# Attention and feed-forward layer on one core: half-width score slots, and transposes of the first 12 cells taken two cells at a time

## The reference, cut to what matters

```python
scores = jnp.einsum('bhqd,bhkd->bhqk', q, k) * scale
causal = jnp.tril(jnp.ones((q_len, q_len), bool))
scores = jnp.where(causal[None, None], scores, jnp.asarray(-1000000000.0, dt))
attn = jax.nn.softmax(scores, axis=-1)
out = jnp.einsum('bhqk,bhkd->bhqd', attn, v)
```

## Time and profile before

| what | before |
|---|---|
| median of 3 runs | 2385.06 us (2380.48 to 2385.91) |
| the profiled execution | 2382.02 us |
| its span, first to last instruction | 2380.2 us |
| PE busy | 2369.0 us |
| ACT busy | 1621.9 us |
| DVE busy | 1430.2 us |
| POOL busy | 579.8 us |
| granted TensorE clock, mean | 1.000 |

### The profile page before, as it was taken

The page is one execution under the profiler, slowest core; times in us unless marked ns, Lnnn a source line. Parts: engine busy times, 40 slices in busy tenths (PEclk is TensorE's granted clock), DMA queues, the critical chain, the costliest instruction groups (busy, mean ns, idle before and its releaser), DMA issues.

```text
span 2380.2 us, 41136 instructions
## 1 busy us (share of the span) xinstructions
PE 2369.0 (100%) x12028; PEld 1993.7 (84%) x12028; DVE 1430.2 (60%) x3796; ACT 1621.9 (68%) x3224; POOL 579.8 (24%) x453
## 2 busy tenths in 40 slices
PE   9999999999999999999999999999999999999998
PEld 7888888888888888888888888888888888888887
DVE  5334666666767676766667676766676675242333
ACT  4223878788888888887878888887888885222221
POOL 3002323233332423232323333232323220000000
PEclk9999999999999999999999999999999999999999
DMA  7867444444353444344444445354444345420110
GB/s 272 303 214 290 131 147 138 132 137 149 137 172 106 171 140 146 128 145 139 135 140 141 142 132 164 118 172 123 160 135 145 129 138 194 140 71 36 53 36 18
DMA packets 133271, 340.24 MB, mean 143 GB/s; under 512 B 13344, under 2 KB 30752, under 8 KB 122656
## 3 DMA queue, kind: packets, MB, share of 16 engines
q1 hardware_dynamic: 133216, 339.53, 42.3%
HBM read 232.00 MB, written 111.67 MB: 144 GB/s over the span
## 4 chain that ended last, share of the span: by engine, by line
PE 96%; issue 1%; DVE 1%; ACT 1%; DMA 1%; SPq 0%; POOL 0%; POOLq 0%; DVEq 0%
PE b_ps L267 45%; PE b_sps L267 34%; PE b_tps L1571 10%; PE b_tps L1630 3%; PE b_ps L1630 3%; PE b_tps L267 1%; DMA a_raw<-in_wkrT 0%; PE b_sps L1580 0%; DMA b_kt<-k_d 0%; ACT b_pt L1068 0%; ACT b_sc L1053 0%; ACT b_sc L1047 0%; DVE b_sc L1272 0%; DVE a_xs L1196 0%; POOL a_wkr L930 0%
## 5 line engine op out<-in xcount | busy, mean ns | idle before, releaser
L1290 DVE TENSOR_TENSOR b_pt<-b_tps,b_pt 128x512 fp32r<-128x512 f32 (+3 forms) x768 | 426.7, 556 | 301.5 <-ACT b_pt L1068 297.2
L267 PE MATMUL b_sps<-b_kt,b_qs 128*128 128x512 f32 (+4 forms) x2304 | 497.1, 343 | 0.2 <-DMA b_kt<-k_d 0.2
L1053 ACT ACTIVATE b_sc<-b_sc,b_rinv 128x896 f32<-128x896 f32 (+7 forms) x512 | 396.1, 774 | 105.4 <-DVE b_rinv L1280 98.8
L267 PEld LDWEIGHTS b_sps<-b_kt,b_qs 128*128 128x128 f32 x2304 | 403.2, 188 | 55.6 <-issue 0.9
L1068 ACT ACTIVATE b_pt<-b_tps 128x512 fp32r<-128x512 f32 (+3 forms) x768 | 367.6, 479 | 115.7 <-PE b_tps L1571 113.9
L267 PE MATMUL b_ps<-b_xs,b_wq 128*128 128x512 f32 x1536 | 440.7, 406 | 0.0
L267 PE MATMUL b_ps<-b_pt,b_vt 128*128 128x512 f32 x1584 | 435.9, 402 | 0.3 <-DVE b_ys L1301 0.3
L267 PE MATMUL b_ps<-b_wo,b_ot 128*128 128x512 f32 x1536 | 423.9, 405 | 0.1
L1047 ACT ACTIVATE b_sc<-b_sc,b_nmax 128x896 f32<-128x896 f32 (+7 forms) x512 | 395.4, 772 | 40.1 <-DVE b_nmax L1272 37.0
L1272 DVE CUSTOM_DVE_ANT_0 b_sc<-b_sps,b_mask 128x896 f32<-128x896 f32 (+7 forms) x512 | 386.5, 755 | 16.2 <-PE b_sps L267 16.1
L1571 PE MATMUL b_tps<-b_ident,b_sc 128*128 128x128 f32 x2304 | 374.3, 272 | 1.4 <-DVE b_pt L1290 1.3
(11 more groups left out here) (142 smaller groups left out, 2274.5 us busy)
## 6 DMA issues: line engine op xcount, KB each, us to landing
b_xs<-xs_d SPq DMA_DIRECT2D x32, 2048.0 KB, 9.0
b_ys<-y_d SPq DMA_DIRECT2D x128, 256.0 KB, 2.7
y_d<-b_ys SPq DMA_DIRECT2D x128, 256.0 KB, 3.0
k_d<-a_ks SPq DMA_DIRECT2D x32, 512.0 KB, 3.9
v_d<-a_vs SPq DMA_DIRECT2D x32, 512.0 KB, 3.0
b_kt<-k_d SPq DMA_DIRECT2D x64, 256.0 KB, 4.3
b_vt<-v_d SPq DMA_DIRECT2D x16, 1024.0 KB, 4.8
b_wraw<-in_wqT SPq DMA_DIRECT2D x64, 256.0 KB, 2.8
```

Of the source, the lines that this page charges most:

```text
L267: ins = nc.tensor.matmul(out, *every[n], start=(n == 0), stop=(n == len(every) - 1))
L1053: nc.scalar.activation(sc[:, slot, 0:w], sc[:, slot, 0:w], ACT.Copy, scale=rinv[:, slot:slot + 1])\
L1290: nc.vector.tensor_tensor(pt[:, u, LO, 0:nj, h * P:(h + 1) * P], tps[n % 2][:, 0:nj], pt[:, u, HI, 0:nj, h * P:(h + 1) * P], ALU.subtract) ...
```

## The change

Two things are changed. Cells 0 to 15 get half a slot (512 columns) of `sc` each, so eight of them fit where four did, and DVE waits for the transposes of cell c - 8 in place of c - 4. And the transposes of cells 0 to 11 are made in steps 4, 6, 8, 10, 12 and 14, those of cells c - 1 and c one behind the other, where each had a step of its own (3 to 14). In steps 3, 5, 7, 9, 11 and 13 PE makes scores and fill alone. ACT and DVE take both pieces in the step of the pair, as their jobs 0 and 1. The diff, cut:

```diff
+PAIRED = 12
+
+
+def transposed_in(step):
+
+    if LAG <= step < PAIRED + LAG:
+        return [(step - LAG - 1, 0), (step - LAG, 0)] if (step - LAG) % 2 else []
+    c = step - LAG
+    return [(c, n) for n in range(len(pieces(c % CELLS)))]
...
+PAIR_ORDER = ("scores", 0, 1, "fill")
...
+        def sc_at(c):
+
+            return sc[:, c % S_RING, 512 * (c // GQ % 2):][:, 0:512] if c < 16 else sc[:, c % S_RING]
+
+        def sc_before(c):
+
+            return c - 2 * S_RING if S_RING <= c < 16 else c - S_RING
...
-                dve.wait_ge(t_done, PIECES * it + thru(c - S_RING) + TD0)
+                dve.wait_ge(t_done, PIECES * it + thru(sc_before(c)) + TD0)
...
-                        elif cell := cell_at(step - LAG, it, turn):
-                            hi_pt(*cell, job)
+                        elif job < len(ts := transposed_in(step)) and (cell := cell_at(ts[job][0], it, turn)):
+                            hi_pt(*cell, ts[job][1])
...
-                    ts = pieces(cell[1]) if cell else []
-                    shares = cut(parts, SHARES[len(ts)])
-                    for job in (0, 1, "scores") if step == 0 else PE_ORDER[part_of(step)]:
+                    ts = [(cell, pieces(cell[1])[n]) for c, n in transposed_in(step) if (cell := cell_at(c, it, turn))]
+                    paired = LAG <= step < PAIRED + LAG
+                    shares = cut(parts, (1,) if paired else SHARES[len(ts)])
+                    order = PAIR_ORDER if paired else PE_ORDER[part_of(step)]
+                    for job in (0, 1, "scores") if step == 0 else order:
```

More of the change, by code:

```diff
@@ L1045, in exp @@
                 act.wait_ge(sc_done, CELLS * it + c + 1 + SC0)
-                nc.scalar.activation(sc[:, slot, 0:w], sc[:, slot, 0:w], ACT.Exp, bias=nmax[:, slot:slot + 1],
+                nc.scalar.activation(sc_at(c)[:, 0:w], sc_at(c)[:, 0:w], ACT.Exp, bias=nmax[:, slot:slot + 1],
                                      scale=-1.0, accum_out=rsum[:, slot:slot + 1]).then_inc(exp_done, 1)
@@ L1052, in normalise @@
                 act.wait_ge(rinv_done, CELLS * it + c + 1)
-                nc.scalar.activation(sc[:, slot, 0:w], sc[:, slot, 0:w], ACT.Copy, scale=rinv[:, slot:slot + 1])\
+                nc.scalar.activation(sc_at(c)[:, 0:w], sc_at(c)[:, 0:w], ACT.Copy, scale=rinv[:, slot:slot + 1])\
                     .then_inc(norm_done, 1)
@@ L1270, in mask_max @@
                 w = P * (i + 1)
[L1272 removed]
+                nc.vector.tensor_tensor_reduce(out=like_banks(sc_at(c)[:, 0:w], i), in0=both_banks(sps[c % 2], i),
                                                in1=like_banks(mask[:, S - w:S], i),
@@ L1440, in turn_of @@
                                     add_q(it + g, int(kind == "q1"), a)
-                        elif cell := cell_at(step - LAG, it, turn):
-                            lo_pt(*cell, job)
+                        elif job < len(ts := transposed_in(step)) and (cell := cell_at(ts[job][0], it, turn)):
+                            lo_pt(*cell, ts[job][1])
                             if turn in ("first", "loop") and step - 1 == D_SPLIT[0] and job == 0:
@@ L1570, in transposes @@
                 for j in range(nj):
-                    last = nc.tensor.transpose(tps[n % 2][:, j], sc[:, c % S_RING, (j0 + j) * P:(j0 + j + 1) * P],
+                    last = nc.tensor.transpose(tps[n % 2][:, j], sc_at(c)[:, (j0 + j) * P:(j0 + j + 1) * P],
                                                ident[:])
@@ L1746, in turn_of @@
                     parts = plan_of(turn).spread[step]
-                    here, cell = cell_at(step, it, turn), cell_at(step - LAG, it, turn)
+                    here = cell_at(step, it, turn)
                     if step == 0:
@@ L1760, in turn_of @@
                         elif job < len(ts):
-                            transposes(*cell, ts[job])
+                            transposes(*ts[job][0], ts[job][1])
             def a_all_values(t):
```

## The result

| | before | after |
|---|---|---|
| median of 6 runs each, same chip | 2382.99 us | 2393.72 us (2392.35 to 2394.59) |
| ratio after / before | | 1.0043, 95% interval 1.003 to 1.0056 |
| span of the profiled execution | 2380.2 us | 2392.5 us |

What follows compares the result with a forecast made beforehand. PE was taken as the bound, busy 2369.0 of 2380.2 us. Gains of 1.0 + 1.9 and cost 0 gave 2.9 us: 2379.1 us profiled, 2382.2 us as median, range 2375 to 2388.5 us.

Steps and rivals of the forecast that it cites:

- Part 3: Moved work on ACT and DVE: same instruction counts, the shifted copies covered by 0.71 us at cell 13; cost 0.
- rival B: New wait at cell 13: shifted ACT copies delay `normalise` by over 0.66 us; 20.8 us lost, 2403 us; chance 0.04.
- Part 2: Cell 0's late transpose in step 3 goes, 2.3 us, less 0.4 charged at cell 1; gain 1.9 us, 1.5 to 2.3.
- Part 1: On PE, 96 merged pairs save a transpose-fill border of 0.01 us each; gain 1.0 us, between 0 and 1.9.
- Rival A: A transpose border on PE costs the visible 0.09 us, so merging saves that; 10.5 us gained, 2374.6 us; chance 0.07.
- Rival C: Nothing gained: borders cost 0.00 and step 3's wait moves whole to cell 1; 2385 us; chance 0.17.
- Rival D: PE's clock falls in longer transpose runs, matmuls taking twice the time; 42 us lost, 2424 us; chance 0.02.
- The base of the sum: Starting times on the kernel before: 2382.0 us for the profiled execution, 2385.1 us for the median of the runs.
- if the even steps show a late transpose: Sign against the forecast: transposes starting late in the even steps, where the pairs stand, would prove it wrong.
- the cell 13 check: Sign in the profile after: cell 13's transpose must follow its `normalise` by more than 0.05 us.

Runs made afterwards that it cites:

- e10: The change, with ACT taking both copies of a pair ahead of `exp` in steps 3 to 14; 2385.04 us, ratio 1.0012 to the kernel before.
- e12: The change, with DVE taking the low part of a pair's second piece one step later, behind reciprocal and `add_q`; 2385.91 us, ratio 1.0012.
- e4: The change, with half of step 15's fill put ahead of the transposes of cell 12; 2394.19 us, ratio 1.0045.
- e5: Kernel before, fill of steps 20 to 31 in four shares, one put amid the first piece's four transposes; 2383.78 us, ratio 1.0003.
- e6: Kernel before, fill of steps 20 to 31 in the same four shares, the first piece left whole; 2383.50 us, ratio 1.0003.
- e3: The change with only cells 0 to 7 in pairs, the last two pairs left out; 2384.63 us, ratio 1.0010.
- e11: The change, with both copies of a pair ahead of `exp` on ACT and half of step 15's fill ahead of cell 12's transposes; 2381.90 us, ratio 0.9994.
- e8: Kernel before, with the four high copies of the `wo` weights moved from ACT to POOL; 2401.42 us, ratio 1.0078.
- e9: The change, with half of the fill ahead of the transposes in steps 15 to 18 (cells 12 to 15); 2394.33 us, ratio 1.0044.

## Why the prediction was wrong, point by point

**Part 3 failed, and with it the forecast.** It said: "0.71 us of cover, of which 0.49 and 0.05 are used, 0.17 left. Cost 0." Three things were wrong in that step.

- It looked at one reader only, cell 13's `normalise`. The reader of piece 10 itself was left out: cell 12's transposes need DVE's low part of piece n - 2, and that rule stands in the text on the kernel. Before, it had 3.37 us; one step later it had less than nothing. It could have been charged ahead of the run, as is worked out below this list.
- It said of DVE that "the low part of the second piece stands ahead of the next step's row maximum" and stopped there. What stands directly behind it is reciprocal and `add_q`, and ACT waits for `add_q`. The copy that was put behind `exp` holds DVE for 0.52 us, and DVE then holds ACT, which the rows show as 0.28 of idle time. This happens in steps 13 and 15 (in front of 925.72 and, with the same 0.28, of 932.82) and pushes all of ACT back. The hold is longer than the idle time: the copy of the queries starts 0.87 us behind the copy ahead of it (924.85 to 925.72), and 0.48 in e10 (920.67 to 921.15). The 0.39 between them is nearly the whole of the 0.41 us a turn that e10 and e12 both give back.
- It treated the 0.49 of the moved copy as the whole shift of `normalise`. In the change `normalise` of cell 13 starts 0.08 us ahead of the scores of step 16 (933.36 and 933.44) where it started 0.54 ahead before (927.59 and 928.13), and PE had itself lost 0.61 by then: 1.07 us later in all, beyond the 0.66 that I had named as the point where rival B decides.

The charge for the reader that was left out: piece 10 gets the place on ACT and DVE that piece 11 had, and the rows of before show that place.

```profile
924.99 0.47 ACT L1068 ACTIVATE b_pt<-b_tps 128x384 fp32r<-128x384 f32 x1
```

```profile
925.50 0.56 DVE L1290 TENSOR_TENSOR b_pt<-b_tps,b_pt 128x384 fp32r<-128x384 f32 x1 [0.44 <-ACT b_pt L1068]
```

DVE ends at 926.06, and cell 12's transposes started at 925.84. With 0.05 us for the semaphore that makes an estimate of 0.27 us a turn, 4 us; e10 shows 0.20, 3 us. Either alone is more than parts 1 and 2 bring.

**Rival B** had the right sign and half of the cause, ACT late by moved copies, but neither the ring nor the nearer reader, and the chance 0.04. Its place was one step off (cell 13's wait comes out only in e4, where the nearer one is taken away) and its price of 20.8 us is twice the loss. The step in which I dismissed it, "the idle time stands ahead of cell 8", looked at ACT's idle time as if ACT were fed by PE alone.

**Part 2** was right on the wait that goes and wrong on what comes next. Step 3 is 0.25 us shorter, as said. But steps 3 and 4 together win only 0.04 us a turn and not 0.12. I had looked for the loss at cell 1's transposes. The timeline of the change in step 4, with DVE's row that belongs to it (L1319 adds a block of the output and so empties a `ps` bank) and the weight loads (PEld):

```profile
901.77 0.69 DVE L1319 TENSOR_TENSOR b_ys<-b_ps,b_ys 128x512 f32<-128x512 f32 x1
901.79 0.51 PE L277 MATMUL b_sps<-b_kt,b_qs 128*128 128x256 f32 x3
...
902.14 0.38 PE L1589 MATMUL b_tps<-b_ident,b_sc 128*128 128x128 f32 x2
...
902.58 0.76 PEld L277 LDWEIGHTS b_ps<-b_pt,b_vt 128*128 128x128 f32 x4
902.60 1.18 PE L277 MATMUL b_ps<-b_pt,b_vt 128*128 128x512 f32 x4
...
903.61 0.51 PE L277 MATMUL b_sps<-b_kt,b_qs 128*128 128x256 f32 x3
```

The same place of that turn before:

```profile
896.93 0.69 DVE L1301 TENSOR_TENSOR b_ys<-b_ps,b_ys 128x512 f32<-128x512 f32 x1
...
897.74 0.82 PEld L267 LDWEIGHTS b_ps<-b_pt,b_vt 128*128 128x128 f32 x4
...
897.90 1.09 PE L267 MATMUL b_ps<-b_pt,b_vt 128*128 128x512 f32 x4
...
898.83 0.52 PE L267 MATMUL b_sps<-b_kt,b_qs 128*128 128x256 f32 x3
```

The pair starts 0.35 us behind the scores, both transposes on time. The four products with the values take 903.61 - 902.60 = 1.01 us to the next scores, where they took 0.93. DVE frees the bank at 902.46 and their first weights are loaded 0.12 later, only 0.02 ahead of the product. Before, the load also came 0.12 behind DVE's row, but 0.16 ahead of the product. That the late load makes a product late is inferred, and no run takes it away; the 0.08 us is read. So by this reading the reader that is late next was the first user of the bank, 1.3 us in all and not 0.4, and part 2 was worth 0.04 x 15 = 0.6 us in place of 1.9.

**Part 1** was about right. The five other pairs of steps are +3, -10, +2, -4 and -42 ns a turn, together 0.05 us less, so 0.8 us in 16 turns against the 1.0 charged. Most of that is one pair, though, and e5 and e6 put a border at 0.0015 to 0.005 us, by which 96 of them are worth 0.1 to 0.5 us: inside the bounds of 0 to 1.9, and below the charge. Rival A is out by these two runs.

**Rival C** (nothing comes of it) is what the kernel would be without the wait: e3 and e11 stand at +1.7 and -1.3 us to the kernel before.

**Rival D** did not come, the granted clock stayed at 1.00. Its price had less under it than it seemed: the first twelve matmuls, from which it was taken, stand in a stretch (2.20 to 6.40 us) for which the profile gives a granted clock of 1.00, so it is not shown that their 0.45 us is the time of the lower level.

The base of the sum was a little off too: the three runs at hand had the median 2385.06 us, all six have 2382.99. That is 2.1 us and changes nothing in the verdict, for the gain of 2.9 was a loss of 10.7.

The signs that the forecast named showed it in part: "if the even steps show a late transpose" was the wrong place (they show none), but the cell 13 check came out at 934.07 to 934.32, 0.25 us, of the 0.70 of before. The range failed since part 3 had cost zero in both of its bounds. A zero with a cover of 0.17 us should have been given a bound of its own.

## What to carry to other kernels

When a job is moved a step later, list for each buffer that it frees or fills the next user and its lead, on every engine, and do the sum for each; the shortest lead decides, and behind it the next one waits. When two engines hand work back and forth in fixed orders, follow the ring once round: a job that waits holds all that stands behind it on its engine, also what the other engine needs in order to be on time. And if an edit that removes a wait gives nothing, look for the next reader of the same late engine (cell 12, cell 13, then the `wo` fill here) before blaming the edit.

## What the runs showed of the hardware

POOL's subtraction for the `wo` weights takes 1.30 us in every one of 64 times before (within 0.02), and in the change 1.30 in 32 and 1.81 in 32 (mean 1551 ns against 1295). The 1.81 belongs to those that run beside DVE's `add_q`. POOL in the change, beside the `add_q` at 925.01 above:

```profile
925.03 1.81 POOL L923 TENSOR_TENSOR b_wo<-b_wraw,b_wo 128x512 fp32r<-128x512 f32 x1 [1.33 <-ACT b_wo L1059]
...
928.17 1.30 POOL L923 TENSOR_TENSOR b_wo<-b_wraw,b_wo 128x512 fp32r<-128x512 f32 x1
```

It begins 0.02 behind the `add_q` and lasts 0.51 longer than the other. All 32 rows of 1.81 us run beside an `add_q`, none of the 32 others does. In e8 it is the other way round: `add_q` starts 0.07 behind POOL's row and takes 1.64 us in place of 0.67. In e10, e11 and e12, where POOL's row no longer starts just behind an `add_q`, the mean is 1294 to 1296 ns again (920.21 and 920.85 are the two starts in e10). The Trainium skill (SBUF — State Buffer, Who interferes with whom) says that a DVE instruction with two SBUF inputs contends with a GpSimd instruction that reads SBUF, and that issue order decides who blocks. The traces agree: the one that starts second is the longer one, POOL by 0.51 us in the change, DVE by 0.97 us in e8. It is no part of the 10.7 us: no row of PE or ACT in the turns waits for POOL in the change, and DVE's waits for POOL are the same in the change and in e10 (41.9 us in 30 times and 11.8 in 19). But it is in the late fill of e9: without the 0.51 the weights would have been there at 936.64, ahead of the 936.93 at which that fill is due.

The other one is how a wait ends on PE, by these two places. Where the low part of a piece came last, the transposes started 0.05 us behind it (931.05 to 931.10); where `normalise` came last, which is waited for one instruction ahead, 0.13 us (936.87 to 937.00). So here the time from the end of the releasing row to the transposes depended on which of the two waits was the later.
